# A scan kernel's first tiles: where q's product, the keys' transposes and the gate product stand

## The chip, the cores and the metric

The kernel runs on one core of a Trainium2 chip. The metric is the device time of one execution in microseconds (us), median of the runs. The five queues that matter are TensorE (PE), VectorE (DVE), ScalarE (ACT), GpSimd (POOL) and SyncE (SP), which issues the DMA transfers. Each executes its own list of instructions in order; they meet only at semaphores.

## The reference, cut to what matters

`x` is 2048 tokens by 512 features in float32; there are 16 heads of 32 features and chunks of 16 tokens.

```
q = silu(ln(x) Wq); k = l2norm(ln(x) Wk); v = ln(x) Wv; beta = 2 sigmoid(ln(x) Wbeta)
for each chunk (128 of them, in order), per head, with a state S of 32 x 32:
    kh = k S;  v_new = gradient of a layer norm of kh against the target v - k
    qh = q S - (tril(q k^T) beta) v_new;  o = q + ln(qh);  S = S - (k beta)^T v_new
gate = ln(x) Wg1 Wg2;  og = rms(o * sigmoid(gate));  x = x + ln((og * norm_w) Wo)
x = x + ln(FFN(ln(x)))         # gate/up/down weights rounded to float8, 512 -> 1536 -> 512
```

The chunks depend on each other through S, so they are a serial chain; all else is work of a tile (128 tokens, 8 chunks) that has to be done beside it.

## The kernel before, in words

There are 16 tiles of 8 chunks. The body for tile `t` is written out once for each engine, for chunk `j` = 0 to 7. In it an engine does the scan's steps of chunk `j` of tile `t`, and around them pieces of three other tiles: the preparation (`prep_*`) of tile t+1, the gating, norm and output product (`post_*`) of tile t-1, and the residual (`tail_*`) and feed-forward part (`ffn_*`) of older ones. The order is the order of the lines: nothing is scheduled at run time. "Tile 1, chunk 0" below is the body with t=1, j=0.

The scan's steps of one chunk run from engine to engine. PE reads the state: `read_state` (L509 keys into bank 0, then L518 queries, which waits until ACT has copied the last chunk's result out of bank 1, `take_qh` L838). DVE and POOL turn kh into `VX` (DVE L1291 to L1327, with POOL's root `rho` L1033 in the middle). PE writes the state: `write_state` (L532, L540). DVE adds it (`scan_state`, `SQ` L1334), and the next chunk's read can begin. On PE every product of the tile's work that stands between a read and a write, or between a write and the next read, is ahead of it in the queue.

The preparation of tile t+1, in the order of the chunks of tile t:

- chunk 0: PE turns the normalized tile (`prep_xnT`, L414), ACT copies it to `xnT` (L730). Where tile t+1 is 1, 2 or 3 (`early`), half of q's product follows at once (`prep_q` with quarters 0 and 1, L407), ahead of the chunk's write; the other half comes in chunk 1.
- chunk 1: ACT takes q (silu, L742), then `take_qh`. DVE turns the gate of tile t (`prep_thR`).
- chunk 2: k's product (L407), after q was taken; q is transposed.
- chunk 3 and 4: POOL's root for the keys' norm, v's product, DVE forms the keys `kn` and `dv`.
- chunk 5: PE transposes the keys into bank 3 (`prep_kT`, L414). DVE makes `kR` from that bank (L1234); it stands behind the chunk's `VX`. ACT then spreads the same bank into `BDk` in two halves of four copies (L783): the first ahead of `take_qh`, the second behind it, with the copies of `g1` and beta between. ACT's first half waits for DVE's `kR`, since two engines would else read one bank at once.
- chunk 6: ACT makes `rT` (L806). PE makes the gate product into bank 3 once both halves of `BDk` are out of it (`prep_gate`, L428), then the centring product from `rT` (`prep_cen`, L434), then the chunk's write. ACT takes the gate (tanh, `prep_th`, L812).
- chunk 7: the output product of tile t-1 goes into bank 3 (`post_wo`, L555), ahead of the chunk's write; it waits for `prep_th` of the tile to come.

The feed-forward weights are rounded while the first tiles run: 36 units, about one a chunk, up to tile 4. A unit passes DVE (`exponent`, L1429), ACT (`magic`, L888 and L890), POOL (`shift`, L1119, after the chunk's `VX`) and DVE (`quantize`, L1439), and then SP loads the one after next. The feed-forward products of tile pairs begin in tile 3; banks 6 and 7, which take their results, are idle until tile 4.

The residual of tile t-2 in an odd tile: POOL's four small steps of `tail_ra` (L1037 to L1042) in chunk 0, ACT's `tail_xc` (L854), which also needs the reload of x (SP, L376), `take_qh`, then DVE's `tail_x1` (L1375).

## Time and profile before

| | us |
|---|---|
| median of 3 runs | 907.01 (906.49 to 908.02) |
| the profiled execution | 907.54 |
| its span in the trace | 905.8 |
| between the two | 1.74 |

| engine | busy us | share of the span |
|---|---|---|
| PE | 794.1 | 88% |
| DVE | 672.2 | 74% |
| ACT | 500.6 | 55% |
| POOL | 488.7 | 54% |

The granted clock of PE has a mean of 0.942 over the span, in tenths of full speed per slice of 22.6 us: 10 9 7 9 6 8 8 8 8 9, then 9 or 10. 1.0 is 2.4 GHz and 0.5 is 1.2 GHz. Tiles 0 to 3 take 28 to 231 us of the span, before the feed-forward products fill PE.

In a line of a timeline stand the start in us from the start of the span, the duration (of the group, where several instructions were merged), the engine, the line, the operation with out<-in, the count, and in brackets the idle time of the engine ahead of it and what ended that. PE's count is twice the products of the code for float32. A PE group's start is that of its first weight load, which can lie under the product before it.

### The profile page before, as it was taken

The page shows a single profiled execution, that of the slowest core. Times are in us where ns is not written, and L with a number is a line of the kernel's source. Part 1 is how long each engine was busy: PE and PEld are TensorE (multiplying, and loading weights), DVE is VectorE, ACT ScalarE, POOL GpSimd, SP SyncE. Part 2 cuts the span into 40 slices and gives each one's busy share as a digit, 9 for nine tenths or more (in the row PEclk, how much of TensorE's full clock was granted, in tenths as well). Part 3 has the DMA queues.
Part 4 walks back from the last instruction along what each step waited for, and adds up shares of the span by engine and source line. Part 5 has one row for each costly group of instructions (what it writes and reads, how often), then busy time and mean ns, then how long its engine had stood idle before and what let it go on. Part 6 is the DMA issues. An engine that isn't in the chain of part 4 may idle for free.

```text
span 905.8 us, 22857 instructions
## 1 busy us (share of the span) xinstructions
PE 794.1 (88%) x8260; PEld 557.1 (62%) x8260; DVE 672.2 (74%) x2693; ACT 500.6 (55%) x1330; POOL 488.7 (54%) x860
## 2 busy tenths in 40 slices
PE   6767776768978999999999999999999999889795
PEld 2344443436656675767676676766766767677594
DVE  2586887888778787878787778788777877866332
ACT  1657575765757555564647465666565555613231
POOL 5354646556546555646565646565655556536222
PEclk9796887888989999999999999999999999989898
DMA  8011021121110001000100010000100010001000
GB/s 267 13 48 59 25 71 36 37 59 36 60 35 25 26 2 47 3 24 2 48 2 25 1 37 14 25 2 5 45 8 19 2 48 2 2 1 48 1 24 24
DMA packets 16720, 28.47 MB, mean 31 GB/s; under 512 B 3520, under 2 KB 3520, under 8 KB 16608
## 3 DMA queue, kind: packets, MB, share of 16 engines
q1 hardware_dynamic: 16608, 27.02, 9.6%
q8 instruction: 65, 1.06, 0.5%
q14 instruction: 47, 0.39, 0.1%
HBM read 22.82 MB, written 4.19 MB: 30 GB/s over the span
## 4 chain that ended last, share of the span: by engine, by line
PE 58%; DVE 15%; POOL 11%; ACT 9%; issue 6%; DMA 0%; POOLq 0%; DVEq 0%; ACTq 0%
PE bank L572 17%; PE bank L407 16%; PE bank L605 8%; PE bank L532 4%; PE bank L555 3%; POOL rho L1033 3%; PE bank L414 3%; ACT BDk L783 3%; PE bank L509 2%; PE bank L518 2%; PE bank L428 2%; PE bank L540 2%; DVE work L1318 2%; DVE kR L1234 1%; DVE work L1322 1%
## 5 line engine op out<-in xcount | busy, mean ns | idle before, releaser
L1033 POOL TENSOR_TENSOR rho<-sy,cst 128x2 f32<-128x2 f32 x128 | 89.5, 699 | 240.1 <-DVE sy L1291 240.1
L1334 DVE TENSOR_TENSOR SQ<-SQ,bank 128x128 f32<-128x128 f32 x128 | 36.8, 287 | 90.9 <-PE bank L532 89.7
L532 PEld LDWEIGHTS bank<-VX,BDkR 128*64 128x64 f32 x1024 | 46.2, 142 | 93.3 <-issue 39.4
L532 PE MATMUL bank<-VX,BDkR 128*64 128x64 f32 x1024 | 57.5, 235 | 41.4 <-DVE VX L1327 41.4
L838 ACT ACTIVATE qhR<-bank 128x64 f32<-128x64 f32 x128 | 28.2, 221 | 108.5 <-PE bank L540 108.1
L605 PE MATMUL bank<-DW,fh 128*128 128x512 f32 x192 | 82.1, 428 | 1.5 <-DVE fl L1401 1.5
L797 ACT ACTIVATE BDkR<-kR,cst 128x128 f32<-128x128 f32 x256 | 81.4, 397 | 0.0
L783 ACT ACTIVATE BDk<-bank 32x256 f32<-32x256 f32 x124 | 46.6, 376 | 58.5 <-DVE kR L1234 50.8
L605 PE MATMUL bank<-DW,fl 128*128 128x512 f32 x192 | 76.8, 400 | 0.0
L1313 DVE SCALAR_TENSOR_TENSOR work<-work,rho,rR 128x32 f32<-128x32 f32 x256 | 53.1, 249 | 26.4 <-POOL rho L1033 25.9
L1114 POOL TENSOR_TENSOR fl<-f,fh 128x512 fp32r<-128x512 f32 x32 | 45.3, 1415 | 50.7 <-ACT fh L730 31.5
L518 PE MATMUL bank<-SQ,BDq 128*64 128x32 f32 x1024 | 54.7, 228 | 17.1 <-ACT qhR L838 15.9
L509 PEld LDWEIGHTS bank<-SQ,BDk 128*64 128x64 f32 x1024 | 46.6, 143 | 37.4 <-issue 33.3
L572 PE MATMUL bank<-xh,GW 128*128 128x256 f32 x384 | 66.0, 295 | 3.6 <-DVE xl L1384 3.5
L572 PE MATMUL bank<-xh,UW 128*128 128x256 f32 x384 | 67.0, 298 | 0.7 <-DVE f L1395 0.7
L407 PE MATMUL bank<-Wq,xnT 128*64 128x512 f32 x256 | 64.3, 642 | 2.1 <-ACT xnT L730 2.1
L407 PE MATMUL bank<-Wv,xnT 128*64 128x512 f32 x256 | 65.2, 630 | 0.0
L509 PE MATMUL bank<-SQ,BDk 128*64 128x48 f32 x1024 | 57.0, 233 | 8.2 <-DVE SQ L1334 6.3
L407 PE MATMUL bank<-Wk,xnT 128*64 128x512 f32 x256 | 63.0, 637 | 0.7 <-ACT xnT L730 0.7
L572 PE MATMUL bank<-xl,GW 128*128 128x256 f32 x384 | 62.7, 286 | 0.0
L555 PE MATMUL bank<-Wo,o 128*64 128x512 f32 x256 | 59.9, 611 | 2.9 <-DVE o L1366 2.9
L572 PE MATMUL bank<-xl,UW 128*128 128x256 f32 x384 | 62.1, 284 | 0.0
(154 smaller groups left out, 2141.5 us busy)
## 6 DMA issues: line engine op xcount, KB each, us to landing
xt<-in_x SPq DMA_DIRECT2D x16, 256.0 KB, 2.9
x<-in_x SPq DMA_DIRECT2D x16, 256.0 KB, 2.7
out<-x SPq DMA_DIRECT2D x16, 256.0 KB, 2.0
yb<-in_gate_w SPq DMA_DIRECT2D x12, 256.0 KB, 2.7
yb<-in_up_w SPq DMA_DIRECT2D x12, 256.0 KB, 2.7
yb<-in_down_w SPq DMA_DIRECT2D x12, 256.0 KB, 2.7
Wk<-in_wk SPq DMA_DIRECT2D x1, 1024.0 KB, 6.5
Wv<-in_wv SPq DMA_DIRECT2D x1, 1024.0 KB, 8.5
```

What stands on the lines that cost most here:

```text
L407: ins = mm(dst[lo, :], half(xnT, k, lo), W[:, k * n:(k + 1) * n], start=(k == 0), stop=(k == KD - 1), skip_group_check=True)
L509: ins = mm(KAv[gp * 64:(gp + 1) * 64, gh, 0:48], bdk(s)[:, gh * NC + j, gp, :], SQv[:, 2 * gh + gp, :], start=True, stop=True, skip_group_ ...
L518: ins = mm(QH[gp * 64:(gp + 1) * 64, gh * DH:(gh + 1) * DH], bdq[:, j // 4, 2 * gp + gh, j % 4, :], S[:, 2 * gh + gp, :], start=(gh == 0), ...
L532: ins = mm(dS[p, e], bdkr[:, gh, j % 4, p], VX[:, e], start=True, stop=True, skip_group_check=True)
L555: ins = mm(PA[1][lo, :], half(ogT, g, lo), Wo[:, g * D:(g + 1) * D], start=(g == 0), stop=(g == 3), skip_group_check=True)
L572: ins = mm(b[:, q * PAIR:(q + 1) * PAIR], W[:, k * I + m * P:k * I + (m + 1) * P], part[:, k * PAIR:(k + 1) * PAIR], start=(part is xh and ...
L605: ins = mm(Y[k][:, :], part[:, q * PAIR + k * P:q * PAIR + (k + 1) * P], DW[:, m * D:(m + 1) * D], start=(m == 0 and part is fh), stop=(m ...
L783: ins = fn(bdk(s)[q, :, gp, own(h)], PA[1][p:p + 32, 256 * a:256 * a + 256].rearrange("p (m c) -> p m c", c=CH), ACT.Copy)
L797: ins = fn(bdkr[:, :, place, h * DH:(h + 1) * DH], kR[:, :].rearrange("p (gh j e) -> p gh j e", gh=2, e=DH)[:, :, js], ACT.Identity, scale ...
L1033: tt(dst, src, cst[:, C_NH:C_NH + n], ALU.pow).then_inc(*one)
L1114: tt(fl[:, :], f[:, :], fh[:, :].bitcast(F32), ALU.subtract).then_inc(*low_g.one("fl"))
L1313: stt(out=g2(g)[:, gh], in0=g2(u)[:, gh], scalar=rho[:, gh:gh + 1], in1=r_j[:, gh, :], op0=ALU.mult, op1=ALU.add).then_inc(*scan_v.one(f"g ...
```

## The change

Six edits, all in the order of work or in the waits; the arithmetic is the same. (1) In tile 0 q's product for tile 1 leaves chunk 0; three quarters stand in chunk 1 ahead of the write, the last behind it. In tiles 1 and 2 it stays. (2) For tiles 1 to 3 the keys are transposed twice, first into bank 7 for DVE's `kR`, then into bank 3 for ACT's `BDk`, and ACT no longer waits for `kR`. (3) For tiles 1 to 3 the gate product leaves chunk 6 of the tile before and stands in chunk 0 of its own tile, behind the transposes of the next tile's x, into bank 6; ACT's tanh moves with it, between `magic` and the square of `post_qsq`. `post_wo` then waits for `BDk`. (4) The wait of k's product for `tail_x1` moves to q's transposes. (5) ACT's `ffn_fh` of chunk 2 goes ahead of `magic`. (6) POOL's `tail_ra` of odd tiles goes ahead of `shift`.

The diff cut to its core, in this order: PE's steps, PE's body, ACT's `prep_BDk`, ACT's body, POOL's body, DVE's `prep_kR`. `PA` are banks 2 and 3, `Y` banks 6 and 7.

```diff
             def prep_k(t):
                 pe.wait_ge(*prep_a.at("q", t))
-                if begun(t - 3):
-                    pe.wait_ge(tail_v.sem, tail_v.at("x1", t - 3))
                 proj(PA[0][:, :], Wk, D).then_inc(*prep_t.one("k"))
             def prep_qT(t):
+                pe.wait_ge(*prep_a.at("q", t))
+                if begun(t - 3):
+                    pe.wait_ge(tail_v.sem, tail_v.at("x1", t - 3))
                 turn(PA[1], qtok, prep_t.one("qT"))
...
             def prep_kT(t):
                 pe.wait_ge(*prep_v.at("d", t))
+                if early(t):
+                    turn(Y[1], kn, prep_t.one("kT2"))
                 turn(PA[1], kn, prep_t.one("kT1"))
...
             def prep_gate(t):
-                pe.wait_ge(*prep_a.at("BDk", t))
-                gate_out(PA[1])
+                if early(t):
+                    pe.wait_ge(*prep_a.at("g1", t))
+                    gate_out(Y[0])
+                else:
+                    pe.wait_ge(*prep_a.at("BDk", t))
+                    gate_out(PA[1])
...
             def post_wo(n):
-                if not isinstance(n, int) or n + 2 < NT:
+                if early(n + 2):
+                    pe.wait_ge(*prep_a.at("BDk", n + 2))
+                elif n + 2 < NT:
                     pe.wait_ge(*prep_a.at("th", n + 2))
...
                     if j == 0:
                         if prep:
                             prep_xnT(t + 1)
-                        if early(t + 1):
+                        if early(t):
+                            prep_gate(t)
+                        if t > 0 and early(t + 1):
                             prep_q(t + 1, (0, 1))
...
                     if j == 1:
-                        if early(t + 1):
+                        if t == 0:
+                            prep_q(1, (0, 1, 2))
+                        elif early(t + 1):
                             prep_q(t + 1, (2, 3))
...
                     if j == 6:
-                        if prep:
-                            prep_gate(t + 1)
                         if early(t + 1):
                             prep_cen(t + 1)
+                        elif prep:
+                            prep_gate(t + 1)
...
                     if j == 1:
+                        if t == 0:
+                            prep_q(1, (3,))
...
                 if a == 0:
                     act.wait_ge(*prep_t.at("kT1", t))
-                    if t > 0:
+                    if t > 0 and not early(t):
                         act.wait_ge(*prep_v.at("kR", t))
...
+                    if j == 2 and 0 in ffn:
+                        ffn_fh(*ffn[0])
                     for u in unit_before(t, j):
                         magic(u)
                     if j == 0:
+                        if early(t):
+                            prep_th(t)
                         if post:
                             post_qsq(t - 1, o)
...
                     if j == 6:
                         if prep and not early(t + 1):
                             prep_rT(t + 1)
-                        if prep:
                             prep_th(t + 1)
...
                     if scan:
                         scan_rho(t, j, s)
+                    if j == 0 and tail and s:
+                        tail_ra(t - 2)
                     if scan and pool_free(t, j):
...
                     if j == 0:
-                        if tail and s:
-                            tail_ra(t - 2)
...
             def prep_kR(t, s):
-                dve.wait_ge(*prep_t.at("kT1" if t else "kT2", t))
+                one, b = ("kT2", PA[0]) if t == 0 else ("kT2", Y[1]) if early(t) else ("kT1", PA[1])
+                dve.wait_ge(*prep_t.at(one, t))
```

Where it moves instructions. PE, tile 0, from q's first product of chunk 0 to chunk 1: L532/L540 are the write, L509/L518 the read (in the changed kernel L539/L547 and L516/L525), L407 with Wq is q. Before:

```order
L407 MATMUL bank2<-Wq,xnT 64x512 [waits prep_a_xnT]
L407 MATMUL bank2<-Wq,xnT 64x512 x3
L532 MATMUL bank0<-VX,BDkR 64x64 [waits scan_v,kdiag_a]
L532 MATMUL bank0<-VX,BDkR 64x64 x3
L540 MATMUL bank1<-VX,ATB 64x32 x4
L509 MATMUL bank0<-SQ,BDk0 64x48 [waits scan_v,chunk_a]
L509 MATMUL bank0<-SQ,BDk0 64x48 x3
L518 MATMUL bank1<-SQ,BDq 64x32 [waits scan_a]
L518 MATMUL bank1<-SQ,BDq 64x32 x3
L407 MATMUL bank2<-Wq,xnT 64x512 x4
L532 MATMUL bank0<-VX,BDkR 64x64 [waits scan_v]
```

Now (the write of chunk 0 begins one row ahead of these):

```order
L539 MATMUL bank0<-VX,BDkR 64x64 x3
L547 MATMUL bank1<-VX,ATB 64x32 x4
L516 MATMUL bank0<-SQ,BDk0 64x48 [waits scan_v,chunk_a]
L516 MATMUL bank0<-SQ,BDk0 64x48 x3
L525 MATMUL bank1<-SQ,BDq 64x32 [waits scan_a]
L525 MATMUL bank1<-SQ,BDq 64x32 x3
L407 MATMUL bank2<-Wq,xnT 64x512 [waits prep_a_xnT]
L407 MATMUL bank2<-Wq,xnT 64x512 x5
L539 MATMUL bank0<-VX,BDkR 64x64 [waits scan_v]
L539 MATMUL bank0<-VX,BDkR 64x64 x3
L547 MATMUL bank1<-VX,ATB 64x32 x4
L407 MATMUL bank2<-Wq,xnT 64x512 x2
```

Four products have left the place ahead of chunk 0's write; six stand ahead of chunk 1's, two behind it.

PE, tile 0, chunk 5: the transposes of the keys `kn`, of `dv`, and the products for g1 and beta. Before, and then now:

```order
L414 MATMUL bank3<-cst,q_kn_th 128x128 [waits prep_v_d]
L414 MATMUL bank3<-cst,q_kn_th 128x128 x3
L414 MATMUL bank4<-cst,xn_dv_rT 128x128 [waits prep_v_d]
L414 MATMUL bank4<-cst,xn_dv_rT 128x128 x3
L421 MATMUL bank2<-xnT,Wgb 64x64 [waits prep_v_kn]
L421 MATMUL bank2<-xnT,Wgb 64x64 x7
L407 MATMUL bank2<-Wgb,xnT 64x16 x8
```

```order
L414 MATMUL bank7<-cst,q_kn_th 128x128 [waits prep_v_d]
L414 MATMUL bank7<-cst,q_kn_th 128x128 x3
L414 MATMUL bank3<-cst,q_kn_th 128x128 x4
L414 MATMUL bank4<-cst,xn_dv_rT 128x128 [waits prep_v_d]
L414 MATMUL bank4<-cst,xn_dv_rT 128x128 x3
L421 MATMUL bank2<-xnT,Wgb 64x64 [waits prep_v_kn]
L421 MATMUL bank2<-xnT,Wgb 64x64 x7
L407 MATMUL bank2<-Wgb,xnT 64x16 x8
```

Four more transposes stand ahead of those that ACT reads, in bank 7. ACT beside them, tile 0, chunk 5, from `magic` over BDk's first half to `take_qh` (before, then now):

```order
L888 ACTIVATE x13<-x13,epses 128x512 [waits s_exp]
L890 ACTIVATE x13<-x13,epses 128x512 [waits s_over]
L783 ACTIVATE BDk1<-bank3 32x16x16 [waits prep_v_kR,prep_t_kT1]
L783 ACTIVATE BDk1<-bank3 32x16x16 x3
L838 ACTIVATE qhR0<-bank1 128x2x32 [waits scan_t]
```

```order
L903 ACTIVATE x13<-x13,epses 128x512 [waits s_exp]
L905 ACTIVATE x13<-x13,epses 128x512 [waits s_over]
L798 ACTIVATE BDk1<-bank3 32x16x16 [waits prep_t_kT1]
L798 ACTIVATE BDk1<-bank3 32x16x16 x3
L853 ACTIVATE qhR0<-bank1 128x2x32 [waits scan_t]
```

The order is the same; the wait for `kR` is gone.

PE, tile 1, chunk 0: transposes of x, gate product (L428), first half of q, write. Before, and then now:

```order
L414 MATMUL bank2<-cst,xn_dv_rT 128x128 [waits prep_v_em,norm_a]
L414 MATMUL bank2<-cst,xn_dv_rT 128x128 x3
L407 MATMUL bank2<-Wq,xnT 64x512 [waits prep_a_xnT]
L407 MATMUL bank2<-Wq,xnT 64x512 x3
L532 MATMUL bank0<-VX,BDkR 64x64 [waits scan_v,kdiag_a]
L532 MATMUL bank0<-VX,BDkR 64x64 x3
```

```order
L414 MATMUL bank2<-cst,xn_dv_rT 128x128 [waits prep_v_em,norm_a]
L414 MATMUL bank2<-cst,xn_dv_rT 128x128 x3
L428 MATMUL bank6<-g1T,Wg2 64x128 [waits prep_a_g1]
L428 MATMUL bank6<-g1T,Wg2 64x128 x7
L407 MATMUL bank2<-Wq,xnT 64x512 [waits prep_a_xnT]
L407 MATMUL bank2<-Wq,xnT 64x512 x3
L539 MATMUL bank0<-VX,BDkR 64x64 [waits scan_v,kdiag_a]
L539 MATMUL bank0<-VX,BDkR 64x64 x3
```

The gate product has come in between the transposes and q, ahead of the write.

## Rows read from the trace of the kernel before

**Rows 1.** Windows of tile 0, tile 3 and later: length, PE, PEld, DVE, ACT, POOL busy, PEclk, DMA.

```profile
28.00:76.90 48.90, 32.68 (x356) 19.42 (x356) 32.06 (x136) 31.36 (x82) 21.50 (x36) 0.79 0.13 34
...
177.80:231.20 53.40, 42.41 (x464) 28.92 (x462) 42.88 (x169) 34.46 (x88) 31.57 (x52) 0.87 0.16 46
300.00:400.00 100.00, 97.67 (x1081) 68.91 (x1082) 79.86 (x334) 59.10 (x169) 56.79 (x107) 1.00 0.06 18
```

**Rows 2.** Timeline, PE, tile 0, chunks 0 to 2: start, us, engine, line, operation [idle before].

```profile
34.25 3.68 PE L407 MATMUL bank<-Wq,xnT 128*64 128x512 f32 x8 [0.69 <-ACT xnT L730]
37.71 0.64 PE L532 MATMUL bank<-VX,BDkR 128*64 128x64 f32 x8
...
39.68 2.02 PE L407 MATMUL bank<-Wq,xnT 128*64 128x512 f32 x8
42.16 0.45 PE L532 MATMUL bank<-VX,BDkR 128*64 128x64 f32 x8 [0.46 <-DVE VX L1327]
...
44.30 3.63 PE L407 MATMUL bank<-Wk,xnT 128*64 128x512 f32 x16
48.36 0.45 PE L532 MATMUL bank<-VX,BDkR 128*64 128x64 f32 x8 [0.43 <-DVE VX L1327]
```

**Rows 3.** Windows, whole core: PEclk is the third number from the end.

```profile
30.00:39.50 9.50, 6.72 (x49) 3.62 (x50) 2.62 (x12) 3.84 (x12) 0.29 (x2) 0.50 0.10 28
77.50:87.50 10.00, 7.95 (x66) 4.92 (x68) 7.19 (x33) 5.52 (x14) 3.68 (x6) 0.50 0.20 62
```

**Rows 4.** Timeline, ACT, tile 0, chunks 5 and 6.

```profile
66.06 1.54 ACT L783 ACTIVATE BDk<-bank 32x256 f32<-32x256 f32 x4 [1.66 <-DVE kR L1234]
...
70.23 1.50 ACT L806 ACTIVATE xn_dv_rT<-bank,wbF,wF 128x128 f32<-128x128 f32 x4
...
73.00 0.58 ACT L812 ACTIVATE q_kn_th<-bank 128x512 f32<-128x512 f32 x1
```

**Rows 5.** Timeline, PE, tile 0, chunk 5.

```profile
61.77 0.66 PE L414 MATMUL bank<-cst,q_kn_th 128*128 128x128 f32 x4 [0.41 <-DVE xn_dv_rT L1251]
...
65.67 0.38 PE L540 MATMUL bank<-VX,ATB 128*64 128x32 f32 x8
```

**Rows 6.** Timeline, POOL, tile 0, chunks 6 and 7.

```profile
73.24 1.27 POOL L1119 TENSOR_TENSOR yb<-x,yb 128x512 f32<-128x512 f32 x1 [3.77 <-ACT x L890]
...
76.45 0.70 POOL L1033 TENSOR_TENSOR rho<-sy,cst 128x2 f32<-128x2 f32 x1
```

**Rows 7.** Timeline, PE, tiles 1 and 2.

```profile
82.84 3.68 PE L407 MATMUL bank<-Wq,xnT 128*64 128x512 f32 x8 [0.69 <-ACT xnT L730]
...
120.01 1.98 PE L428 MATMUL bank<-g1T,Wg 128*64 128x128 f32 x16 [1.66 <-ACT BDk L783]
...
125.40 3.64 PE L555 MATMUL bank<-Wo,o 128*64 128x512 f32 x16
...
132.12 1.94 PE L407 MATMUL bank<-Wq,xnT 128*64 128x512 f32 x8 [0.69 <-ACT xnT L730]
```

**Rows 8.** Timeline, DVE, tile 1 chunk 0 and tile 2 chunk 0.

```profile
84.52 0.29 DVE L1327 TENSOR_TENSOR VX<-work,re 128x128 f32<-128x128 f32 x1
...
134.96 0.29 DVE L1334 TENSOR_TENSOR SQ<-SQ,bank 128x128 f32<-128x128 f32 x1
```

**Rows 9.** Timeline, POOL, tile 3, chunk 0.

```profile
186.10 1.27 POOL L1119 TENSOR_TENSOR yb<-x,yb 128x512 f32<-128x512 f32 x1 [1.20 <-DVE VX L1327]
...
188.37 0.19 POOL L1042 TENSOR_TENSOR nb_a<-nm_a,rs_a 128x1 f32<-128x1 f32 x1
```

**Rows 10.** Timeline, ACT, tile 3, chunk 0.

```profile
188.65 0.72 ACT L854 ACTIVATE x<-x,nb_a 128x512 f32<-128x512 f32 x1 [2.60 <-POOL nb_a L1042]
```

**Rows 11.** Timeline, PE, tile 3, chunk 1.

```profile
189.98 5.36 PE L407 MATMUL bank<-Wq,xnT 128*64 128x512 f32 x16
```

**Rows 12.** Timeline, SP, tile 3: the reload of x for tail_xc.

```profile
183.88 0.43 SPq L376 DMA_DIRECT2D x<-in_x  x1
```

**Rows 13.** Tile x, 120 to 260 us: time from issue to landing of its loads.

```profile
DMA to landing us min/median/max: 3.3/3.5/3.6
```

More of the change, by code:

```diff
@@ L458, in prep_k, with prep_qT @@
                 pe.wait_ge(*prep_a.at("q", t))
+                proj(PA[0][:, :], Wk, D).then_inc(*prep_t.one("k"))
+            def prep_qT(t):
+                pe.wait_ge(*prep_a.at("q", t))
                 if begun(t - 3):
                     pe.wait_ge(tail_v.sem, tail_v.at("x1", t - 3))
-                proj(PA[0][:, :], Wk, D).then_inc(*prep_t.one("k"))
-            def prep_qT(t):
                 turn(PA[1], qtok, prep_t.one("qT"))
@@ L811, in prep_th @@
                 act.wait_ge(*prep_t.at("gate", t))
-                fn(thT[:, :], PA[1][:, :], ACT.Tanh, scale=0.5).then_inc(*prep_a.one("th"))
+                fn(thT[:, :], (Y[0] if early(t) else PA[1])[:, :], ACT.Tanh, scale=0.5).then_inc(*prep_a.one("th"))
             def diag_q(n, half, s):
@@ L946, in body @@
                     if j == 2:
-                        if 0 in ffn:
-                            ffn_fh(*ffn[0])
                         if tail and not s:
@@ L1253, in prep_kR @@
             def prep_kR(t, s):
-                dve.wait_ge(*prep_t.at("kT1" if t else "kT2", t))
+                one, b = ("kT2", PA[0]) if t == 0 else ("kT2", Y[1]) if early(t) else ("kT1", PA[1])
+                dve.wait_ge(*prep_t.at(one, t))
                 if begun(t - 1):
                     dve.wait_ge(kdiag_a.sem, kdiag_a.at("k3", t - 1))
-                turn(kR, PA[1] if t else PA[0], prep_v.one("kR"))
+                turn(kR, b, prep_v.one("kR"))
             def prep_rR(t, s, b=None):
```

## The prediction

> **What bounds the kernel now.** I read the page's first part, then windows tile by tile, then the timelines of all engines over the first four tiles.
>
> PE is the busiest engine over the span, 88% in the table above, but the windows split it in two. From 300 us on PE works 97.67 of 100 us at the full clock. In tile 0 it works 32.68 of 48.90 us at a mean granted clock of 0.79, in tile 3 42.41 of 53.40 at 0.87 [rows 1]. There no engine is full: the serial chain of the scan sets the time, through whichever engine holds it. What the change saves there should go through to the end one for one, since behind it every queue runs the same list, and PE, nearly full, merely begins earlier.
>
> So the question is what the chain waits for at the places that move. Four kinds of place: (a) tile 0, chunks 0 to 2, where q's product stands ahead of the write; (b) chunk 5 of tiles 0 to 2, where ACT waits for DVE; (c) chunk 0 of tiles 1 to 3, to which gate and tanh go; (d) chunk 0 of tile 3, with the residual.
>
> **(a) Tile 0, q out of chunk 0.** Before, the transposes of x end at 34.25 - 0.69 = 33.56, q's first half runs 3.68 us, and chunk 0's write starts at 37.71 [rows 2], without having waited for VX. Now the write starts at about 33.56: 4.15 us earlier. Chunk 1's read goes with it, and q would start at 39.68 - 4.15 = 35.53.
>
> There three quarters, 12 matmul instructions, are ahead of chunk 1's write. Eight of them take 3.68 us at the low clock and 2.02, overlap included (about 1.9), at the full one [rows 2]: 0.46 and 0.24 each. The granted clock is 0.50 from 30 to 39.5 us [rows 3], after an almost idle PE, and rises while q runs. Three cases:
> - It stays low to the end: 12 x 0.46 = 5.5, end 41.05.
> - It rises at 39.5 as before: 3.97 us give 8.6 instructions, 3.4 x 0.24 = 0.8 are left, end 40.3.
> - It rises some 3 us sooner, since the 0.69 us of idle time ahead of q [rows 2] is filled by write and read: end about 38.8.
>
> Before, chunk 1's write starts at 42.16, just behind VX [rows 2]; VX comes 4.15 sooner, at 38.0, and does not bind. Behind it k's product starts 2.14 us later, at 44.30 [rows 2]. Now q's last quarter (0.45) and the silu (0.6) lie in that stretch in place of ACT's older work; I take 2.25. k takes 3.63, so chunk 2's write comes 2.25 + 3.65 = 5.9 us behind chunk 1's and now waits for PE, where before it came 6.20 behind (48.36 - 42.16) and waited 0.43 for VX. It comes at 46.95, 46.2 or 44.7 instead of 48.36. The gain is **1.4, 2.15 or 3.65 us; I take 2.7**, near the middle of the last two.
>
> **(b) Chunk 5, the keys in two banks.** Before, ACT sits idle for 1.66 us until kR, starts BDk's first half at 66.06 and then copies qh [rows 4]. The transposes for it were done at 61.77 + 0.66 = 62.4 [rows 5]. Now a second set is ahead: 0.6 more, 63.0, still far below the 64.40 at which ACT comes free (66.06 - 1.66). So the first half runs 64.40 to 65.94. The chunk's last products end at 65.67 + 0.38 = 66.05 [rows 5], and ACT's qh copy can start there, where before it started at 67.6. All of ACT's list behind comes 1.54 us sooner, less 0.05: g1, beta, BDk's second half, rT (70.23) [rows 4], magic. POOL's shift sat idle for 3.77 us for magic and started at 73.24; POOL's steps behind it end in the root of chunk 7 at 76.45, with no idle time between [rows 6]. So the whole 1.5 reaches chunk 7. PE's write of chunk 6 follows the centring product, which waits for rT at 70.23 + 1.50 = 71.7; the gate product, done meanwhile, cost nothing there and brings nothing by leaving. The tanh that leaves ACT (0.58 [rows 4]) is behind magic and brings nothing either. Tiles 1 and 2 have the same pattern, and the same wait for BDk ends ahead of the gate product at 120.01 [rows 7]. **3 x 1.5 = 4.5 us.** The bounds of each: 0 if the early half of BDk ends behind the chunk's products and only swaps places with qh; 2.4 if the centring product ran at the full clock and POOL did not bind.
>
> The extra transposes (12 of them) lie in a wait of PE for VX: nothing.
>
> **The output product.** In tiles 1 and 2 it stands in chunk 7 ahead of the write. Before, gate and centring products (the first from 120.01, 1.98 us at the low clock) ran ahead of it, and it ran 3.64 us, 16 instructions, all at the full clock from 125.40 [rows 7]. Now only the centring product is ahead, and it starts 1.5 us earlier, at 123.9; the clock rose at about 125.2. The 1.3 us before that yield 2.8 instructions at 0.46 instead of at 0.23: 0.65 more. Bounds 0 and the whole 1.5. **Loss 0.5 each, 1.0 in all.**
>
> The Trainium skill, TensorE: Matmul & The Clock Gate, Part 1: "the default state is throttled, and activity releases the throttle". It speaks against this edit, since the gate product was activity; by it the output product could lose all of the 1.5, and that is the first rival below.
>
> **(c) Gate and tanh in chunk 0.** Tile 1: the transposes of x end at 82.84 - 0.69 = 82.15; the gate product takes 1.98 us at the low clock, about 1.8 without the overlap at its end [rows 7], and q's half starts at 83.95 instead of 82.84. At the low clock (0.50 from 77.5 to 87.5 [rows 3]) the write comes 1.1 us later. But the 0.69 us gap is filled. If the clock rises for that, q takes 1.94 as in tile 2 [rows 7] and ends at 85.9 or before, no sooner than VX at 84.81 [rows 8]; DVE's state step also stands behind the sum of squares that waits for ACT's tanh and square, so the gain is 1.0 at most. **I take +0.2, bounds -1.1 and +1.0.** Tile 2: q's half starts at 132.12 at the full clock [rows 7]; the gate takes 1.0 there, 0.7 of it in the gap, and the write is just about where it was. At the low clock it would cost 2.4. The tanh (0.6 on ACT) pushes the square and DVE's sum, and the state step at 134.96 follows directly behind that sum [rows 8]: **-0.4.** Tile 3 has no q here; its PE is idle behind the transposes.
>
> **(d) Tile 3, the residual.** ACT's tail_xc waits 2.60 us for POOL, to 188.65 [rows 9, 10], behind a shift of 1.27 us that itself waited 1.20 for VX. With POOL's four steps ahead of the shift, nb_a is there 2.5 us sooner, at 188.56 - 2.47 = 186.1. What is late next is the reload of x: issued at 183.88 [rows 12], 3.5 us to landing [rows 13], so 187.4. And ACT's list has the tanh ahead, to 186.7, so that does not bind. 188.65 - 187.4 = 1.25 us for qh and tail_x1. Behind them q's 5.36 us, mostly at the low clock [rows 11], hold the write; they may take more of their time at the low clock. **+1.1, bounds 0.3 and 1.3.** The shift is pushed by nothing: it waits for VX, which ends after nb_a would.
>
> The moved wait in k, and `ffn_fh`: k waits for q's silu, which is later than tail_x1 in each tile I looked at, and DVE shows no wait for fh. Nothing.
>
> **Sum.** 2.7 + 4.5 - 1.0 + 0.2 - 0.4 + 1.1 = 7.1 us. The profiled execution is 907.54 (905.8 and 1.74 outside), 0.5 above the median of 907.01; it becomes 900.4, the median 899.9.
>
> **The rivals.**
> 1. The clock takes it. Output products lose all of (b) in tiles 1 and 2 (2.0 more), tile 1's chunk 0 loses 1.1 (1.3 more), and tile 0 has the low clock throughout (1.3 more): 904.5. For it: PE's clock is low just where work moves [rows 3]. Against it: no gain in (b) depends on PE. Chance 0.12.
> 2. BDk only swaps places with qh, because the first half ends late by more than the 0.1 us of room (65.94 against 66.05): 4.5 falls away, 904.4. Against it: kR's wait was the only thing ahead. Chance 0.07.
> 3. The clock rises early at each place: 3.65 in place of 2.7, 1.0 of 0.2, no loss in the output products, 2.75 more: 897.2; and down to 895.5 where the centring product runs at the full clock too. Chance 0.08.
> 4. Slower: without the gate product in chunk 6 the clock stays low right through tile 1's and tile 2's output products. One then takes 7.0 us, twice 3.5, from 123.9 to 130.9, where before it ended at 125.40 + 3.64 = 129.0 [rows 7]: 1.9 us lost instead of 1.5 won. The gate product and q's half behind it run low too. Before, q's half began 3.1 us behind the output product and ended at 134.06 [rows 7]; now it ends at 130.9 + 3.1 - 0.7 + 1.8 + 3.68 = 138.8, of which 0.4 had been slack: 4.3 lost in all. Then 1.9 more in tile 2; tile 0 gives 1.4 + 1.5, tile 1's chunk 0 costs 1.1, tile 3 gives 0.3. That is 4.1 slower, 911.1. It decides from the point at which the low clock outlasts the output product; in the trace it ended just ahead of it. Chance 0.03.
> 5. The change does nothing to the end, as something with its own pace holds tile 4: nothing in the windows has one. Chance 0.02.
>
> **Chances and range.** The forecast, 898 to 903, has 0.68. The range, 895.5 to 904.5, holds it with rival 3 and about half of rivals 1 and 2, and leaves out their slower halves, 4 and 5. A measurement of this kernel tells 0.2% (1.8 us) from no change. Faster by over that, below 905.2: 0.92; within it 0.05; slower 0.03.
>
> **What the changed profile would show.** (a) chunk 0's write starts near 33.6, with q behind it, and chunk 2's near 45.5. (b) ACT's BDk does not wait for DVE in tiles 0 to 2, and the qh copy comes right behind the chunk's products. (c) gate product in tile 1's chunk 0 with q's half behind it at either clock. (d) tail_xc ends its wait with the reload of x, not with nb_a. The output products: longer than 3.64 us. Wrong it would be if q's half of tile 1's chunk 0 (82.84 before [rows 7]) came less than 2 us sooner, or if what is won by 231 us were not there at the end.

## The result and the profile after

The changed kernel takes **902.33 us**, median of five runs (899.93 to 903.35); the kernel before, run on the same chips, takes 908.02 (906.49 to 909.2). The ratio is 0.9932, 95% interval 0.9911 to 0.9953: faster by 0.68%, some 6.2 us. The forecast was 899.9 in a range of 895.5 to 904.5. The profiled execution took 902.37, its span 900.5 (before 907.54 and 905.8).

I read the changed profile with one measure. DVE's first step of each chunk takes the statistics of the state (`sy<-bank`, L1291 before, L1308 now). Its start in the first chunk of tile 0 is the zero of each trace, since what lies ahead differs from run to run, with no edit in it. From the timeline of DVE, before and then after:

```profile
28.81 0.24 DVE L1291 BATCH_NORM_STATS2 sy<-bank 128x6 f32<-128x68 f32 x1 [1.66 <-PE bank L509]
```

```profile
30.13 0.24 DVE L1308 BATCH_NORM_STATS2 sy<-bank 128x6 f32<-128x68 f32 x1 [1.65 <-PE bank L516]
```

"2.3" is tile 2, chunk 3. The table gives how much sooner (us, minus sign) each such start comes than in the kernel before, both from their own zero. "after" and "again" are two traces of the changed kernel; the others are the experiments below.

| tile.chunk | after | again | q only | keys only | gate only | residual only | fill | reload | both |
|---|---|---|---|---|---|---|---|---|---|
| 0.1 | -4.16 | -4.16 | -4.16 | 0.00 | -0.20 | 0.01 | -4.16 | -4.52 | -4.17 |
| 0.3 | -3.56 | -3.33 | -3.02 | 0.00 | -0.21 | 0.01 | -3.51 | -3.87 | -3.57 |
| 0.6 | -3.71 | -3.47 | -3.15 | -0.13 | -0.12 | -0.02 | -3.66 | -4.01 | -3.70 |
| 0.7 | -5.22 | -4.98 | -3.16 | -1.64 | -0.12 | -0.03 | -5.18 | -5.53 | -5.20 |
| 1.0 | -5.44 | -4.97 | -3.16 | -1.87 | -0.13 | -0.03 | -5.17 | -5.76 | -5.20 |
| 1.1 | -6.45 | -5.97 | -3.16 | -2.00 | -1.02 | -0.03 | -6.18 | -6.76 | -6.20 |
| 1.6 | -6.61 | -6.13 | -2.72 | -2.55 | -0.69 | 0.00 | -6.43 | -6.89 | -6.49 |
| 1.7 | -8.10 | -7.64 | -2.72 | -4.05 | -0.69 | -0.01 | -7.92 | -8.39 | -7.97 |
| 2.0 | -7.56 | -7.09 | -2.61 | -3.73 | -0.64 | 0.00 | -7.91 | -7.83 | -7.97 |
| 2.3 | -7.55 | -7.08 | -2.62 | -3.74 | -0.59 | -0.01 | -7.81 | -7.82 | -7.87 |
| 2.5 | -6.90 | -6.44 | -2.20 | -3.20 | -0.22 | 0.00 | -6.98 | -7.17 | -7.07 |
| 2.7 | -8.35 | -7.89 | -2.19 | -4.65 | -0.21 | 0.00 | -8.43 | -8.63 | -8.51 |
| 3.0 | -7.60 | -7.13 | -2.23 | -4.69 | -0.25 | 0.00 | -8.47 | -7.86 | -8.55 |
| 3.1 | -8.23 | -7.45 | -2.23 | -4.69 | -0.25 | -1.22 | -9.20 | -10.08 | -10.77 |
| 3.2 | -7.51 | -6.88 | -2.25 | -3.94 | -0.31 | -0.60 | -9.59 | -10.30 | -11.16 |
| 4.4 | -7.00 | -6.48 | -2.30 | -3.40 | -0.40 | -0.17 | -9.91 | -10.43 | -10.10 |
| 15.7 | -6.83 | -6.32 | -2.35 | -3.16 | -0.47 | -0.14 | -9.95 | -10.41 | -10.00 |

The last row is what each kernel won by the last chunk: 6.83 and 6.32 us, against 7.1 forecast. From tile 4 on nothing moves by more than 0.5: PE works 97.39 of 100 us there, as before [rows 1]. Windows of the changed kernel (length, PE, PEld, DVE, ACT and POOL busy, granted clock, DMA share, GB/s), tile 0 shortened by what it won:

```profile
29.32:72.78 43.46, 29.49 (x344) 18.31 (x344) 31.98 (x135) 30.41 (x81) 21.27 (x36) 0.80 0.14 38
300.00:400.00 100.00, 97.39 (x1074) 68.70 (x1072) 78.99 (x331) 57.74 (x162) 57.85 (x103) 1.00 0.05 17
```

Tile 0 lost 5.44 us of length; its clock is 0.80 where it was 0.79.

**Why the times differ by less than the table.** The first chunk itself began at 30.13 instead of 28.81. PE's product for k, the first large one, waited for its weights:

```profile
8.75 3.68 PE L407 MATMUL bank<-Wk,xnT 128*64 128x512 f32 x8 [0.69 <-ACT xnT L730]
```

```profile
10.04 2.83 PE L407 MATMUL bank<-Wk,xnT 128*64 128x512 f32 x6 [1.95 <-DMA Wk<-in_wk]
```

The edits don't touch that load. In three of ten traces of this study the product waits for ACT and begins at 8.57 to 8.75, in seven for `Wk` and begins at 9.77 to 10.58; chunk 0 begins between 28.37 and 31.51. The spans of the two profiled executions differ by 5.3 us, and from their zeros they differ by 6.8: of the 1.5 between, this start is 1.3. The medians differ by 5.7 with an interval of 4.3 to 8.1, which holds the 6.8 too. The starts differ by about as much as one run of the changed kernel from another; that they are the cause of that scatter is not shown, since only profiled runs tell their start.

### The profile page after: what moved, and what is told of

Read it like the earlier page. It is cut to its first block, busy times and chain, and to the rows that moved or that the text cites. A ratio compares the mean times of both kernels' runs of the same rounds, so it can differ in the third digit from the quotient of the medians.

```text
span 900.5 us, 22880 instructions
## 1 busy us (share of the span) xinstructions
PE 790.5 (88%) x8272; PEld 557.7 (62%) x8272; DVE 672.6 (75%) x2693; ACT 500.2 (56%) x1330; POOL 488.9 (54%) x860
## 3 DMA queue, kind: packets, MB, share of 16 engines
q8 instruction: 66, 1.08, 0.5%
## 4 chain that ended last, share of the span: by engine, by line
PE 61%; DVE 14%; POOL 9%; ACT 8%; issue 5%; DMA 2%; SPq 0%; POOLq 0%; DVEq 0%; ACTq 0%
PE bank L581 18%; PE bank L407 16%; PE bank L614 8%; PE bank L564 4%; PE bank L539 4%; PE bank L414 3%; POOL rho L1049 3%; PE bank L516 3%; PE bank L525 2%; ACT BDk L798 2%; PE bank L547 2%; PE bank L428 1%; DVE work L1335 1%; PE bank L434 1%; DVE f L1412 1%
## 5 line engine op out<-in xcount | busy, mean ns | idle before, releaser
L539 PEld LDWEIGHTS bank<-VX,BDkR 128*64 128x64 f32 x1024 | 45.9, 141 | 87.9 <-issue 38.0
L539 PE MATMUL bank<-VX,BDkR 128*64 128x64 f32 x1024 | 57.1, 233 | 38.5 <-DVE VX L1344 38.5
L516 PEld LDWEIGHTS bank<-SQ,BDk 128*64 128x64 f32 x1024 | 46.5, 143 | 38.0 <-issue 34.0
L525 PE MATMUL bank<-SQ,BDq 128*64 128x32 f32 x1024 | 54.9, 228 | 14.5 <-ACT qhR L853 13.3
L407 PE MATMUL bank<-Wv,xnT 128*64 128x512 f32 x256 | 65.3, 631 | 0.0
L516 PE MATMUL bank<-SQ,BDk 128*64 128x48 f32 x1024 | 57.0, 232 | 8.1 <-DVE SQ L1351 6.2
L407 PE MATMUL bank<-Wk,xnT 128*64 128x512 f32 x256 | 61.8, 627 | 2.0 <-DMA Wk<-in_wk 2.0
L407 PE MATMUL bank<-Wq,xnT 128*64 128x512 f32 x256 | 61.9, 622 | 0.0
```

Of the source, the lines that this page charges most:

```text
L407: ins = mm(dst[lo, :], half(xnT, k, lo), W[:, k * n:(k + 1) * n], start=(k == 0), stop=(k == KD - 1), skip_group_check=True)
L516: ins = mm(KAv[gp * 64:(gp + 1) * 64, gh, 0:48], bdk(s)[:, gh * NC + j, gp, :], SQv[:, 2 * gh + gp, :], start=True, stop=True, skip_group_ ...
L525: ins = mm(QH[gp * 64:(gp + 1) * 64, gh * DH:(gh + 1) * DH], bdq[:, j // 4, 2 * gp + gh, j % 4, :], S[:, 2 * gh + gp, :], start=(gh == 0), ...
L539: ins = mm(dS[p, e], bdkr[:, gh, j % 4, p], VX[:, e], start=True, stop=True, skip_group_check=True)
```

## The experiments

Each was timed beside the kernel before on the same chip. The first four do one part of the change alone; with intervals of 0.2 to 0.4% from end to end, their traces say more than their times.

### q's product alone (edit 1)

```diff
-                        if early(t + 1):
+                        if t > 0 and early(t + 1):
                             prep_q(t + 1, (0, 1))
...
+                        if t == 0:
+                            prep_q(1, (0, 1, 2))
+                        elif early(t + 1):
                             prep_q(t + 1, (2, 3))
...
                     if j == 1:
+                        if t == 0:
+                            prep_q(1, (3,))
...
```

> The kernel before with the first edit alone: in tile 0 q's product leaves chunk 0, three quarters stand ahead of chunk 1's write, one behind it. Chunk starts are counted from the start of tile 0, chunk 0, against the kernel before. My theory: 4.15 us are won at chunk 1, some given back at chunk 2's write because k's product now holds it, 2.7 us (1.4 to 3.65, by when the clock rises) are left at chunk 3 and stay to the end: about 904.5. Rival: the product only moves its cost to chunk 1, where the write waits for six products instead of four, and less than 1 us is left at chunk 3: 907 or more.

Measured: 904.81, ratio 0.9963 (0.9944 to 0.9981). Chunk 0.1 comes 4.16 sooner, 3.15 are left by chunk 6 and 2.35 at the end. The changed kernel keeps 3.71 in one trace and 3.47 in the other by chunk 6. PE's timeline of the changed kernel (start, us, line, operation, idle time before):

```profile
34.81 0.70 PE L539 MATMUL bank<-VX,BDkR 128*64 128x64 f32 x8
...
36.84 3.27 PE L407 MATMUL bank<-Wq,xnT 128*64 128x512 f32 x12
39.94 0.41 PE L539 MATMUL bank<-VX,BDkR 128*64 128x64 f32 x8
...
42.49 3.63 PE L407 MATMUL bank<-Wk,xnT 128*64 128x512 f32 x16
45.96 0.40 PE L539 MATMUL bank<-VX,BDkR 128*64 128x64 f32 x8
```

Three quarters of q take 3.27 us, since the clock rises while they run. The next write starts 5.13 us behind chunk 0's. In the kernel with this edit alone, the same place:

```profile
38.21 3.82 PE L407 MATMUL bank<-Wq,xnT 128*64 128x512 f32 x12
41.85 0.41 PE L532 MATMUL bank<-VX,BDkR 128*64 128x64 f32 x8
```

The granted clock rises 7.7 us behind the zero in the changed kernel, 8.2 in its second trace and 8.8 with this edit alone, and the three keep 3.71, 3.47 and 3.15; with the filler below it is 7.8 and 3.66. In the kernel before it is 11.1. The instructions are the same: what differs is the moment at which the clock rises, and each us later costs about half a us. Why that moment differs between two traces of one kernel is not shown. The rise at 7.7 is the third of the prediction's cases, some 3 us sooner than before. Chunk 2's write stands right behind k's product, as the prediction had it.

### The keys in two banks alone (edit 2)

```diff
+                if early(t):
+                    turn(Y[1], kn, prep_t.one("kT2"))
                 turn(PA[1], kn, prep_t.one("kT1"))
...
-                    if t > 0:
+                    if t > 0 and not early(t):
                         act.wait_ge(*prep_v.at("kR", t))
...
```

> The kernel before with the second edit alone: for tiles 1 to 3 the keys are transposed into two banks and ACT does not wait for kR. The gate product stays in chunk 6. My theory: 1.5 us at chunk 7 of each of tiles 0, 1 and 2, and, as the gate product still runs ahead of the output product, little of it given back in chunk 7: about 4.2 us at the end, 903.5. Rival 1: BDk's first half only swaps places with the qh copy: nothing at chunk 7, 907.7. Rival 2: the output product runs low for being earlier, whatever stands ahead of it: 0.5 to 0.75 us given back in chunk 7 of tiles 1 and 2 here too, 904.7.

Measured: 906.09, ratio 0.9976 (0.9960 to 0.9991). The three steps are there: 1.51 from chunk 0.6 to 0.7, 1.50 from 1.6 to 1.7, and 1.45 from 2.5 to 2.7; smaller ones between them add 1.1, half of it from 1.1 to 1.6, which I have not traced. At the end it keeps 3.16 of that, 1.0 less than expected: 0.32 goes in tile 1's output product, 0.54 in tile 2's chunks 3 to 5, 0.75 in tile 3's q product, 0.8 behind that. So the second rival on record, an output product that runs low for being earlier, holds behind tile 1 and not behind tile 2. In the changed kernel, ACT in tile 0:

```profile
61.29 0.72 ACT L905 ACTIVATE x<-x,epses 128x512 f32<-128x512 f32 x1
61.92 1.52 ACT L798 ACTIVATE BDk<-bank 32x256 f32<-32x256 f32 x4
63.71 0.22 ACT L853 ACTIVATE qhR<-bank 128x64 f32<-128x64 f32 x1 [0.28 <-PE bank L547]
```

BDk stands directly behind ACT's own work, with no wait; qh comes behind the chunk's products, after 0.28 us of waiting. The prediction's second rival, that the two only swap places, is out.

### Gate and tanh in their tile's first chunk alone (edit 3)

```diff
+                        if early(t):
+                            prep_gate(t)
                         if early(t + 1):
                             prep_q(t + 1, (0, 1))
...
                     if j == 6:
-                        if prep:
-                            prep_gate(t + 1)
                         if early(t + 1):
                             prep_cen(t + 1)
+                        elif prep:
+                            prep_gate(t + 1)
...
```

> The kernel before with the third edit alone: the gate product and its tanh in chunk 0 of their own tile, bank 6; the keys in one bank as before. My theory: nothing at chunk 7 of tile 0 and at most 0.3 us in tiles 1 and 2, since rT binds there; in chunk 7 of tiles 1 and 2 the output product starts at the low clock and loses 0.5 to 1.5 us each; tile 1's chunk 0 moves by between +1.1 and -1.0 with the clock: 907 to 909.5. Rival: the gate product held the chain in chunk 6 (1.8 us at the low clock), and its leaving gives over 1 us in each of tiles 0 to 2: under 905.

Measured: 908.82, ratio 0.9999 (0.9985 to 1.0014): no difference that the timing shows; 0.47 sooner in the trace. What was expected of the output products did not come: they run at the full clock, 3.65 us in tile 1 and 3.64 in tile 2, and nothing over 0.05 is lost behind them.

```profile
124.42 3.65 PE L561 MATMUL bank<-Wo,o 128*64 128x512 f32 x16
```

But tile 1's chunk 0 gives 0.89 (from -0.13 to -1.02), where I had taken 0.2, and the same step is 1.01 in the changed kernel. PE there in the kernel with the keys alone (gate product where it was), and then in the changed one:

```profile
80.78 1.12 PE L414 MATMUL bank<-cst,xn_dv_rT 128*128 128x128 f32 x4
82.59 3.60 PE L407 MATMUL bank<-Wq,xnT 128*64 128x512 f32 x8 [0.69 <-ACT xnT L732]
```

```profile
77.07 1.12 PE L414 MATMUL bank<-cst,xn_dv_rT 128*128 128x128 f32 x4
78.11 1.41 PE L428 MATMUL bank<-g1T,Wg 128*64 128x128 f32 x16
79.36 1.88 PE L407 MATMUL bank<-Wq,xnT 128*64 128x512 f32 x8
81.07 0.40 PE L539 MATMUL bank<-VX,BDkR 128*64 128x64 f32 x8
```

With the gap of 0.69 us, q runs 3.60 at the low clock; with the gate product in it, q runs 1.88 at the full one. With this edit alone it is 1.98, where the kernel before has 3.68 [rows 7]:

```profile
83.28 1.98 PE L407 MATMUL bank<-Wq,xnT 128*64 128x512 f32 x8
```

So the edit brings the full clock forward. The gap by itself does not decide: in tile 2 of the kernel before it stands ahead of a q that takes 1.94 [rows 7]. In the changed kernel the granted clock is 0.55 from 77 to 79 and 1.00 from 79 to 87, where before it was 0.50 for ten microseconds [rows 3]. The write then follows q directly, 1.01 us sooner than before, and DVE becomes the next to be waited for (PE's read of chunk 0 waits 0.56 for `SQ`, behind a sum of squares that waits 0.53 for ACT's `o`).

### The residual alone (edit 6)

```diff
+                    if j == 0 and tail and s:
+                        tail_ra(t - 2)
                     if scan and pool_free(t, j):
...
                     if j == 0:
-                        if tail and s:
-                            tail_ra(t - 2)
```

> The kernel before with POOL's four steps of the residual ahead of the shift in odd tiles, nothing else. My theory: the reload of x is late next, so tail_xc in tile 3, which waited 2.60 us for POOL, now waits about 1.3 us less and ends its wait with that reload; chunk 1 of tile 3 starts 1.2 us sooner, and part of it is lost to q's product at the low clock: 0 to 1.2 us at the end, 906.5 to 908. Rival: POOL alone held it: chunk 1 of tile 3 starts 2.5 us sooner, 905.5.

Measured: 907.62, ratio 0.9995 (0.9983 to 1.0007). ACT's `tail_xc` now waits for the reload, which lands 3.5 us behind its issue, as in my theory:

```profile
187.28 0.72 ACT L854 ACTIVATE x<-x,nb_a 128x512 f32<-128x512 f32 x1 [1.37 <-DMA x<-in_x]
```

Tile 3's chunk 0 wins 1.22 us, chunk 1 gives back 0.62, and 0.14 is there at the end. q's product in tile 3's chunk 1 takes it, 5.98 us instead of 5.36 [rows 11]:

```profile
188.62 5.98 PE L407 MATMUL bank<-Wq,xnT 128*64 128x512 f32 x16
```

### The changed kernel once more

The same kernel as the one predicted, beside the three below.

> The changed kernel once more, to have its chunk starts beside the three below on one chip. Counted from the start of tile 0, chunk 0, as in the first trace: 3.6 to 3.7 us won at chunk 3 of tile 0, 1.5 at chunk 7 of tiles 0 to 2, some 0.5 and 0.75 given back by the output products, 6.8 at the end, about 901.5. If the giving back is an accident of the clock's phase, it differs by more than 0.5 us here.

Measured: 901.64, ratio 0.9929 (0.9910 to 0.9949), 6.32 us at the last chunk. The steps repeat to 0.1 us but for four: 0.1 to 0.3, 0.7 to 1.0, tile 3's chunk 0 (0.32 won where the other trace has 0.63) and its chunk 1 (0.57 lost for 0.72).

### A product for nobody in chunk 6

The gate product of before's place comes back as filler, into bank 6, beside the real one in chunk 0. Nobody reads it; the output is unchanged.

```diff
                         if early(t + 1):
+                            pe.wait_ge(*prep_a.at("g1", t + 1))
+                            for m in range(4):
+                                for lo in HALVES:
+                                    mm(Y[0][lo, m * P:(m + 1) * P], half(Wg2, m, lo), g1T[:, :], start=True, stop=True,
+                                       skip_group_check=True)
                             prep_cen(t + 1)
```

> The changed kernel with the gate product done a second time, in its old place in chunk 6 of tiles 0 to 2, into bank 6, where nobody reads it; it only waits for g1. My theory: PE stands idle there, so the product costs nothing, and its activity lets the clock rise before the output product, which then runs 3.64 us at the full clock: the 0.5 us at tile 2, chunk 0 and the 0.75 at tile 3, chunk 0 come back, and the centring product may run faster: about 1 us faster than the changed kernel. Rival: the output product is late for another reason (it stands ahead of the write whatever the clock): no change, or slower, since the extra product delays chunk 6's write.

Measured: **899.05**, ratio 0.9901 (0.9881 to 0.9922); 2.6 us less than the changed kernel beside it, with no run of the one in the range of the other, and more than the 1 us expected. PE in tile 2's chunks 6 and 7, changed kernel and then filled:

```profile
165.57 1.98 PE L434 MATMUL bank<-xn_dv_rT,cst 128*64 128x512 f32 x4 [3.28 <-ACT xn_dv_rT L821]
...
169.30 4.47 PE L564 MATMUL bank<-Wo,o 128*64 128x512 f32 x16
173.58 0.41 PE L539 MATMUL bank<-VX,BDkR 128*64 128x64 f32 x8
```

```profile
161.85 1.10 PE L680 MATMUL bank<-g1T,Wg 128*64 128x128 f32 x16
165.34 1.08 PE L434 MATMUL bank<-xn_dv_rT,cst 128*64 128x512 f32 x4 [2.38 <-ACT xn_dv_rT L826]
...
168.49 3.66 PE L564 MATMUL bank<-Wo,o 128*64 128x512 f32 x16
172.35 0.45 PE L539 MATMUL bank<-VX,BDkR 128*64 128x64 f32 x8 [0.19 <-DVE VX L1349]
```

Windows of the same stretch (the granted clock is the third number from the end), changed kernel and then filled:

```profile
164.00:171.00 7.00, 5.32 (x40) 2.84 (x42) 6.16 (x27) 5.25 (x14) 4.86 (x10) 0.51 0.17 47
```

```profile
164.00:171.00 7.00, 4.71 (x48) 2.33 (x50) 5.94 (x27) 5.30 (x14) 5.02 (x12) 1.00 0.21 54
```

At the full clock the centring product takes 1.08 instead of 1.98, the output product 3.66 instead of 4.47, and between chunk 7 of tile 2 and chunk 0 of tile 3 nothing is lost, where the changed kernel loses 0.75. In tile 1 the loss goes from 0.54 to 0.01 too, though its output product still takes 4.59 there: it begins 0.81 sooner from the zero, since the centring product ran at the full clock. So the loss of the output products is the clock, and the filler takes it away. The missing gate product alone does not make it: with edit 3 alone, where it is missing too, nothing is lost at either place. Nor does the earlier start alone behind tile 2: with the keys alone, where the product is still ahead, nothing is lost there, and behind tile 1 0.32 of the 0.54. Only the two together give 0.54 and 0.75. The filler also shortens the low stretch at tile 3's q product: the clock rises at 184.6 instead of 188.0, q takes 4.92 us instead of 6.09, and chunk 3.1 to 3.2 wins 0.39 instead of losing 0.72.

### The reload of x a tile sooner

The load that `tail_xc` of tile 3 needs is issued in tile 2, next to that of the tile before it.

```diff
-                    sp.dma_start(x1[n % 4][:, :], x_t[n]).then_inc(s_xr[n % 4], 16)
+                    if n != 1:
+                        sp.dma_start(x1[n % 4][:, :], x_t[n]).then_inc(s_xr[n % 4], 16)
+                    if n == 0:
+                        sp.dma_start(x1[1][:, :], x_t[1]).then_inc(s_xr[1], 16)
```

> The changed kernel with one load moved: the reload of x for the residual of tile 1 (the one that tile 3 uses) is issued in tile 2, beside that of tile 0. My theory: tail_xc in tile 3 then waits for nobody, chunk 1 of tile 3 starts 1.3 to 1.9 us sooner than in the changed kernel, and half of it or more is left behind q's product at the low clock: 0.5 to 1.5 us at the end. Rival: the copy of qh and not the reload holds chunk 1, or the low clock takes all: under 0.3 us at chunk 2.

Measured: **899.08**, ratio 0.9902 (0.9881 to 0.9922), 2.6 us less than the changed kernel where at most 1.5 was expected. ACT in tile 3, changed kernel and then with the early load; SP's issue in the changed kernel between them:

```profile
179.67 0.59 ACT L745 ACTIVATE xnT<-bank 128x512 f32<-128x512 f32 x1
181.74 0.72 ACT L869 ACTIVATE x<-x,nb_a 128x512 f32<-128x512 f32 x1 [1.48 <-DMA x<-in_x]
```

```profile
177.60 0.43 SPq L376 DMA_DIRECT2D x<-in_x  x1
```

```profile
179.71 0.59 ACT L748 ACTIVATE xnT<-bank 128x512 f32<-128x512 f32 x1
180.18 0.72 ACT L872 ACTIVATE x<-x,nb_a 128x512 f32<-128x512 f32 x1
180.80 0.22 ACT L856 ACTIVATE qhR<-bank 128x64 f32<-128x64 f32 x1
```

The wait of 1.48 us for the load is gone, and qh comes 1.57 sooner. PE's part of the same place, changed kernel and then with the early load:

```profile
183.07 6.09 PE L407 MATMUL bank<-Wq,xnT 128*64 128x512 f32 x16
188.99 0.40 PE L539 MATMUL bank<-VX,BDkR 128*64 128x64 f32 x8
```

```profile
181.40 5.26 PE L410 MATMUL bank<-Wq,xnT 128*64 128x512 f32 x16
186.47 0.42 PE L542 MATMUL bank<-VX,BDkR 128*64 128x64 f32 x8
```

q starts 1.67 sooner and takes 0.83 less: the clock is low over less of it. The low clock ends at 184.7 here and at 188.0 there. So chunk 3.2 stands at -10.30 instead of -7.51, and at the last chunk the lead over the changed kernel is 3.6 us; 0.3 of it was there in tile 0 already, where this edit isn't, and by the medians it is 2.6.

### Both

The two edits above together.

> The changed kernel with the second gate product in chunk 6 and the earlier reload together. My theory: both gains add, 1.5 to 2.5 us faster than the changed kernel, about 899.5. Rival: what one gives the clock takes from the other: not faster than the better of the two alone.

Measured: 898.75, ratio 0.9902 (0.9875 to 0.9928): no better than either alone, as the rival had it. Chunk 3.2 stands at -11.16, the best of all, but 3.3 at -9.13, and the end at -10.00. PE behind it:

```profile
187.35 1.55 PE L417 MATMUL bank<-cst,xn 128*128 128x128 f32 x8 [0.41 <-ACT xn L883]
188.83 4.83 PE L410 MATMUL bank<-Wk,xnT 128*64 128x512 f32 x16
```

k's product, 3.65 us in the kernel with the early load alone, takes 4.83. q's product ahead of it runs 3.66, all at the full clock, and the low stretch, about 181.2 to 184.7 with either edit alone, now lies from 187.8 to 191.2, over the transposes and half of k's product. So the two gains share one low stretch of the clock; with both edits it falls on the next product. And not all that q saves arrives: the write behind it now waits 1.28 us for `VX`. A filler there was not tried.

## Why the prediction was right, step by step

**The frame** held in the main. What is won in tiles 0 to 3 goes to the end, less 0.7: 7.51 at tile 3's chunk 2, 6.83 at the last one. The parts alone add to 2.35 + 3.16 + 0.47 + 0.14 = 6.12, all of them together give 6.83 and 6.32: nearly additive. They stand at different places of one chain, but what the clock takes back differs from kernel to kernel, so that the sum comes so near is in part luck. Edits 4 and 5 were not run alone; no step of the traces points to them.

**(a) Tile 0, 2.7 forecast, 3.7 and 3.5 measured** (3.15 alone). The 4.15 at chunk 0 came as 4.16. The mis-sized term is the time of three quarters of q and what stands between the writes: 5.13 us. I took a value between a clock that rises as before and one that rises early; in the traces with this edit it rose 7.5 to 8.8 us behind the zero, where before it was 11.1.

**(b) Chunk 5, 4.5 forecast, 4.45 measured** (1.51, 1.49, 1.45). Each link was as described. This is the largest term and the surest. No part of it depends on the clock: with the filler the centring product of tiles 1 and 2 runs at the full clock, and the steps are still 1.49 and 1.45, so the upper bound of 2.4, for which POOL was not to bind, is out.

**The output products, -1.0 forecast, -1.29 measured** (-0.54 and -0.75). The mechanism is shown by the fill, which takes both away. Weighed against it was the Trainium skill, TensorE: Matmul & The Clock Gate, Part 1, "the default state is throttled, and activity releases the throttle": the rows bear it out in direction, but the loss is some 44% of what (b) wins here, not all of it, as the first rival had it. I had sized it by a clock that rises when it did before. In tile 1 it rose 6.8 us sooner (96.4 us behind the zero before, 89.6 now), while the product began 8.0 sooner, and on the whole this cost little more. That the size came near is luck in part.

**(c) Chunk 0, +0.2 forecast, +1.01 and +1.00 measured in tile 1.** Here the term was mis-sized to its upper bound. I had named the filled gap as what could raise the clock, and weighed it as one case of two. In tile 2 nothing happened: 2.0 to 2.1 moves by 0.01. The 0.4 that I had charged there for tanh ahead of the square was a wrong step. ACT has no wait ahead of tanh and ends the square at 127.49 + 0.62 = 128.11, when DVE ends VX, so DVE does its sum without waiting:

```profile
127.01 0.58 ACT L827 ACTIVATE q_kn_th<-bank 128x512 f32<-128x512 f32 x1
127.49 0.62 ACT L860 ACTIVATE o<-qhR 128x512 f32<-128x512 f32 x1
```

```profile
127.79 0.29 DVE L1344 TENSOR_TENSOR VX<-work,re 128x128 f32<-128x128 f32 x1
128.14 0.69 DVE L1355 TENSOR_REDUCE qss<-o 128x16 f32<-128x512 f32 x1
```

**Not in the sum at all:** from 2.3 to 2.5 the changed kernel loses 0.65. Every variant that is earlier at that place loses there, with the filler 0.83, with the keys alone 0.54, with q alone 0.42, with the gate alone 0.37, and 0.01 with the residual alone, where nothing is earlier. PE before, and then now:

```profile
154.64 0.45 PE L532 MATMUL bank<-VX,BDkR 128*64 128x64 f32 x8 [3.19 <-DVE VX L1327]
...
156.12 4.39 PE L407 MATMUL bank<-Wv,xnT 128*64 128x512 f32 x12
```

```profile
148.41 0.70 PE L539 MATMUL bank<-VX,BDkR 128*64 128x64 f32 x8 [3.24 <-DVE VX L1344]
...
150.43 4.50 PE L407 MATMUL bank<-Wv,xnT 128*64 128x512 f32 x12
```

Write and read ahead of v's product run at the low clock now. Before, the clock was low from 142 to 149, mostly under k's product (6.48 us), and again from 156 to 159; now it is low from 137 to 140 and from 147 to 154. So the longer stretch comes second: k's product takes 5.22, which wins nothing (2.1 to 2.3), and the write and the read take 2.02 us up to v's start instead of 1.48. Why they changed places is open.

**(d) The residual, +1.1 forecast, -0.1 measured.** The wait moved to the reload, as said, but chunk 0 won 0.63 instead of 1.25: the reload took 4.1 us to land (4.4 in the second trace), and I had taken 3.5, which it does take with this edit alone. Why it took longer is open. The second step that failed is the one behind it: I noted that q's product "may take more of their time at the low clock" and charged nothing for it. It took 0.73 more (6.09 for 5.36), and tile 3's gain was gone. Alone, the edit gained 1.22 and lost 0.62 in the same way. A further 0.7 goes from 3.2 to the end, in three steps of 0.2 to 0.3 (at 3.7, at 4.4 and in tile 6). With the keys alone all three are there, with the residual alone the first two, with q or the gate alone none. I have not traced these.

So the sum of 7.1 was near because errors cancel: (a) gave 1.0 more, (c) 0.8 and 0.4; the output products 0.3 less, tile 2's v 0.65, (d) 1.2, and the steps behind it 0.7; small steps along the way bring 0.4. Of the mis-sized terms, all whose cause is known are products at one of the two clocks, but for the tanh and half of (d), the reload. The rivals: the first happened in part (the output products, v, q in tile 3) and the third in part (q in tile 0 and tile 1), at different places of one run. The fourth, slower, did not come near: the low clock never outlasted an output product, the longest of which, 4.59 us with the fill, is far from the 7.0 supposed.

## What to carry to other kernels

An engine's wait that is removed (two copies of a small transpose, so that two readers need not queue) pays in full at its place where the chain is serial, and could be forecast there (1.5 us each; 1.51, 1.49 and 1.45 came). What reaches the end is less certain: here the clock took part of it back. A large product in such a stretch costs 3.7 or 1.9 us for the same eight instructions, according to what TensorE did ahead of it, so ask of each moved product whether it leaves a gap or fills one. A product of no use can be worth more than it costs: here three of 1.1 us each, in idle time of TensorE, gave 2.6 us. Two such gains need not add: if both come from the clock, try them together.

## What the runs showed of the hardware

- At tile 1's q, a gap of 0.69 us ahead of it goes with 3.60 to 3.68 us for its eight instructions, a product in the gap with 1.88 to 1.98. I had thought it possible, not likely. In tile 2 the same gap goes with 1.94 [rows 7].
- The low clock moves rather than vanishes: with q's product in tile 3 kept at the full clock, k's behind it runs 4.83 instead of 3.65.
- The first large product waits for its weights, with 1.9 to 2.6 us idle ahead of it, in seven traces of ten and not at all in three. Chunk 0 starts 1.1 to 3.1 us later in the seven, more than edits 3 and 6 bring together; the wait alone does not set it, since the latest product (10.58) goes with a start at 30.42 and another (10.35) with the latest start, 31.51.
- The 256 KB reload of tile 3, issued right behind another load of its size, landed 4.1 and 4.4 us after its issue in the two traces of the changed kernel (177.60 to 181.74 in the first), where it took 3.6 in the kernel before, issued in the same order, and 3.5 with edit 6 alone.
